# Expert stage of a gated attention and mixture-of-experts block: silu as one function, the row remainder on VectorE, rounding one step earlier, four row buffers, sums formed in the residual's buffer

## The chip, the cores and the metric

The kernel runs on one core of one Trainium2 chip. The metric is device time in microseconds (us) of one execution, the median of several runs. A core has five engines with instruction streams of their own: TensorE (PE, matrix products), VectorE (DVE), ScalarE (ACT), GpSimd (POOL) and SyncE (SP), which here only issues DMAs. They meet through semaphores alone. SBUF holds tiles of 128 partitions; PSUM holds what TensorE writes.

## What is computed

The inputs are 128 sequences of 128 rows of 256 numbers. A gated window attention gives x1. What the change touches is the second half:

```
x = x + tanh(g_xattn[0]) * attention(layernorm(x), ctx)            # x1
x = x + tanh(g_ffn[0]) * ffn(layernorm(x), ...)

def ffn(x, w_router, w_fc, w_gate, w_proj):        # E = 16 experts, K = 2
    gate_probs = softmax(x @ w_router)
    top_k_probs, positions, indices, expert_inputs = dispatch(x, gate_probs)   # 16 rows of a sequence to each expert
    gg = einsum('enc,ech->enh', expert_inputs, w_gate)
    h  = einsum('enc,ech->enh', expert_inputs, w_fc)
    h  = silu(gg) * h
    o  = einsum('enh,ehc->enc', h, w_proj)
    return sum over k of top_k_probs[k] * o[indices[k], positions[k]]
```

All of it is in fp32 accuracy: an operand of a product is split into a rounded head (`_hi`) and a remainder (`_lo`), and three products stand for one.

## The kernel before

Three blocks run one after the other: attention (to about 1310 us of the trace), routing (to about 1340), and the expert block, which the change is in. Attention and routing leave in DRAM the normed rows `xn2_d` and the residual `x1_d`, and in SBUF the tables `place`, `collect_row` and `weight`.

The expert block is a pipeline of steps u = -13 to 141. A step does one unit of each stage, and each stage has a lag: it works at step u on sequence (or expert pair) u minus its lag. The lags are `LOAD -13` (SP fetches the rows of a sequence), `PICK -11` (ACT rounds them to `x_hi`, POOL forms `x_lo`, DVE the selection matrix `pick`), `DISPATCH -9` (PE sorts rows to experts into `DS`, ACT and DVE split that into `s_hi`, `s_lo`), `GATE 0` (PE multiplies by both first weights into `GU`; ACT and DVE form silu(g)*h), `HIDDEN 2` (PE transposes into `HT`, ACT and DVE split it), `OUTPUT 3` (PE multiplies into `EO`, ACT copies it to `eo` and stores it to `eo_d`), `FETCH 12` (POOL gathers the two expert rows of each row of a sequence, `first` and `second`, by an indirect DMA each; SP loads the residual `xr`), and `COLLECT 14` (DVE adds both, weighted, to the residual in `y_sb`; SP stores it). Eight units of GATE to OUTPUT work on one group of eight sequences, two experts each, so a gather of a group waits until all sixteen experts' rows of the group have landed in `eo_d`.

Within a step each engine's instructions stand in the order in which the code is written; nothing is scheduled. All buffers are small rings: three for `x_in_sb` and `xr` (slices of one tile named `scaled`, which the trace shows for both and for `y_sb`), two for `y_sb`, `x_hi`, `x_lo` and the PSUM tiles, three for `eo`, `first` and `second`. So a transfer or an instruction also waits for the last reader of its slot:

- L1129 to L1133, SP: the load for sequence n waits until `x_hi` and `x_lo` of n-3 are done, and stands behind the store of the same step (L1124 to L1126), which waits for `out_done`.
- L1151, POOL: a pair of gathers waits until the sum of n-3 is done; the gathers are followed by `x_lo` (L1162).
- L1188 to L1190, ACT: `x_hi` waits for its load, and the tanh of GATE (L1195) stands behind it.
- L1228 and L1243, DVE: the two sums, with `th` and `hid` (L1235, L1239) between them; the first waits for both gathers, for the residual, and for the store of n-2.

silu(g)*h is computed as (1 + tanh(g/2)) * g * h, with the missing half put into `weight` by the routing block.

## Time and profile before

| what | value |
|---|---|
| median of 3 runs | 1836.87 us (1833.91 to 1838.42) |
| the profiled execution's own time | 1835.99 us |
| its span, first to last instruction | 1834.2 us |
| PE / DVE / ACT / POOL busy over the span | 83% / 77% / 62% / 59% |
| expert block | 1340 to 1834 us |
| its steps without sums (before 1402 us) | PE busy all the time |
| its steps with sums (1402 to 1758 us) | DVE busy 91 to 94%, POOL 80 to 85%, PE 87 to 95% |
| its end (1800 to 1834 us) | gathers on POOL, sums on DVE |

A share of busy time is a mean over unlike stretches. The last third of the run is the expert block, and in it a step is the unit to think in: it has 24 matmuls on PE (12 for GU, 4 for DS, 6 for EO, 2 for HT), so that a count of matmuls in a stretch, divided by 24, is a count of steps.

### The profile page before, as it was taken

Reading aid. Unit: us, or ns where it says so; the run is one execution under the profiler, and the core shown is the slowest. Engines: PE = TensorE matmul, PEld = TensorE weight load, DVE = VectorE, ACT = ScalarE, POOL = GpSimd, SP = SyncE. Lnnn points to the kernel's source line nnn. Section 1 sums busy time; section 2 is a strip of 40 time slices with the busy share of each in tenths; the row PEclk is TensorE's granted clock in tenths of the full one; section 3 lists DMA queues with packets and bytes.
Section 4 is the critical chain, followed back from the end, with each engine's and each line's share of the span. In section 5 each row is a group of like instructions: output and inputs, shape, how many; then the busy total and the mean of one; then the engine's idle time right before and its main releaser. Section 6 shows DMA issues by size and latency. Waiting matters only on the chain. (4 is left out here: it accounts for less than half of the span.)

```text
span 1834.2 us, 50716 instructions
## 1 busy us (share of the span) xinstructions
PE 1520.0 (83%) x16843; PEld 1222.3 (67%) x16844; DVE 1410.9 (77%) x2993; ACT 1133.7 (62%) x2321; POOL 1088.1 (59%) x1490
## 2 busy tenths in 40 slices
PE   4888889988899898898988989986169888898871
PEld 3666666666666666666666666664059888898871
DVE  3777787777877777777777777775968999999964
ACT  3667667677666766766766767674236555565540
POOL 3455465555655555555555555551826888788866
PEclk9999999999999999999999999997569999999995
DMA  2112122121221211212212122242026888898876
GB/s 90 48 58 86 57 71 72 57 86 57 69 74 57 85 58 57 86 57 73 70 57 86 57 70 73 70 145 81 6 72 198 260 263 261 262 286 269 263 228 207
DMA packets 156096, 210.21 MB, mean 115 GB/s; under 512 B 18688, under 2 KB 104832, under 8 KB 156032
## 3 DMA queue, kind: packets, MB, share of 16 engines
q1 hardware_dynamic: 125312, 142.36, 24.5%
q0 software_dynamic: 12288, 33.57, 6.4%
q10 hardware_dynamic: 18432, 33.56, 5.1%
q8 instruction: 24, 0.39, 0.1%
q14 instruction: 40, 0.33, 0.1%
HBM read 125.54 MB, written 83.89 MB: 114 GB/s over the span
## 5 line engine op out<-in xcount | busy, mean ns | idle before, releaser
L505 DVE TRANSPOSE_TENSOR_REDUCE part_max<-ST 128x16 f32<-128x512 f32 x512 | 321.3, 685 | 171.9 <-PE ST L684 168.4
L360 ACT ACTIVATE probs_t<-ST 128x512 f32<-128x512 f32 x512 | 262.5, 596 | 68.2 <-PE ST L699 68.2
L711 PE MATMUL PO<-probs_t,v_aug 128*32 128x128 f32 x4096 | 205.2, 298 | 108.6 <-ACT probs_t L360 95.0
L288 POOL TENSOR_TENSOR ct_lo<-c_in_sb,ct_hi 128x512 fp32r<-128x512 f32 x64 | 82.4, 1288 | 278.0 <-ACT ct_hi L378 278.0
L711 PEld LDWEIGHTS PO<-probs_t,v_aug 128*32 128x32 f32 x4096 | 94.4, 114 | 204.5 <-ACT probs_t L360 192.6
L437 ACT ACTIVATE xn<-x_in_sb,off,rstd 128x256 f32<-128x256 f32 x128 | 70.0, 594 | 224.7 <-POOL off L284 224.7
L1190 ACT ACTIVATE x_hi<-scaled 128x256 fp32r<-128x256 f32 x128 | 53.5, 418 | 210.9 <-DMA scaled<-xn_d 131.9
L1259 PE MATMUL GU<-we_hi,s_hi 128*128 128x256 f32 x512 | 155.8, 304 | 0.0
L1153 POOL DMA_INDIRECT first<-eo_d,collect_row x128 | 126.0, 984 | 44.4 <-issue 24.0
L316 POOL TENSOR_TENSOR q_rest<-q_rot,q_head 128x512 f32<-128x512 f32 x64 | 82.4, 1288 | 112.7 <-ACT q_head L413 112.7
L1153 POOL DMA_INDIRECT second<-eo_d,collect_row x128 | 122.6, 958 | 42.3 <-issue 38.7
L1260 PE MATMUL GU<-we_hi,s_lo 128*128 128x256 f32 x512 | 145.2, 284 | 0.0
L1261 PE MATMUL GU<-we_lo,s_hi 128*128 128x256 f32 x512 | 145.1, 283 | 0.0
L1162 POOL TENSOR_TENSOR x_lo<-scaled,x_hi 128x256 fp32r<-128x256 f32 x128 | 115.2, 900 | 48.8 <-ACT x_hi L1190 46.7
L1259 PE MATMUL EO<-we_hi,h_hi 128*128 128x256 f32 x256 | 82.5, 322 | 53.2 <-issue 39.4
L366 ACT ACTIVATE out_t<-PO 128x512 f32<-128x512 f32 x128 | 78.6, 614 | 71.0 <-PE PO L711 71.0
L729 PE MATMUL F<-ident_sb,xn 128*128 128x128 f32 x512 | 91.8, 306 | 31.6 <-ACT xn L437 19.7
L679 PE MATMUL ST<-q_hi,k_hi 32*128 32x256 f32 x1024 | 94.6, 358 | 5.9 <-issue 5.4
L1260 PEld LDWEIGHTS GU<-we_hi,s_lo 128*128 128x128 f32 x512 | 98.6, 192 | 0.0
L1261 PEld LDWEIGHTS GU<-we_lo,s_hi 128*128 128x128 f32 x512 | 98.1, 192 | 0.0
L1259 PEld LDWEIGHTS GU<-we_hi,s_hi 128*128 128x128 f32 x512 | 97.9, 191 | 0.2 <-issue 0.2
L1259 PEld LDWEIGHTS EO<-we_hi,h_hi 128*128 128x128 f32 x256 | 49.0, 191 | 72.9 <-issue 63.2
(158 smaller groups left out, 5565.7 us busy)
## 6 DMA issues: line engine op xcount, KB each, us to landing
eo_d<-eo ACTq DMA_DIRECT2D x128, 256.0 KB
x_in_sb<-x SPq DMA_DIRECT2D x64, 256.0 KB, 2.8
c_in_sb<-ctx_t SPq DMA_DIRECT2D x64, 256.0 KB, 2.8
xr_sb<-x SPq DMA_DIRECT2D x64, 256.0 KB, 4.0
x_d<-x SPq DMA_DIRECT2D x64, 256.0 KB, 4.1
xn_d<-xn SPq DMA_DIRECT2D x64, 256.0 KB, 4.2
scaled<-xn_d SPq DMA_DIRECT2D x128, 128.0 KB
scaled<-x_d SPq DMA_DIRECT2D x128, 128.0 KB
```

The costliest lines, as they stand in the source:

```text
L288: pool.tensor_tensor(ct_lo[:].rearrange("p k b t -> p (k b t)"), c_in_sb[:, n.par].rearrange("p k b t -> p (k b t)"), ct_hi[:].rearrange(" ...
L316: pool.tensor_tensor(q_rest[:].rearrange("p k t -> p (k t)"), q_rot[:].rearrange("p k t -> p (k t)"), q_head[:].rearrange("p k t -> p (k t ...
L360: act.activation(probs_t[:, b, i].rearrange("p j q -> p (j q)"), ST[i][:], ACT.Exp) \
L505: dve.tensor_reduce(part_max[:, i, 0], ST[i][:].rearrange("p (c l) -> p c l", l=32), AX_X, ALU.max, apply_transpose=True).then_inc(M["part ...
L679: pe.matmul(ST[i][:, m * 2 * SEQ:(m + 1) * 2 * SEQ], k_part[rows, n.par, m, b], q_part[rows, n.par, m, b].rearrange("p e t -> p (e t)"), s ...
L711: last = pe.matmul(PO[32 * j:32 * j + 32, i * SEQ:(i + 1) * SEQ], v_aug[:, n.par, b, head], probs_t[:, b, i, j], start=True, stop=True)
L729: last = pe.transpose(F[:, (2 * k + b) * SEQ:(2 * k + b + 1) * SEQ], src[:, b, k * P:(k + 1) * P], ident[:])
L1153: pool.indirect_dma_start(out=dst[:, n.turn(3)], out_offset=None, in_=D["eo_d"][n.group].rearrange("r e c -> (r e) c"), in_offset=bass.Ind ...
L1162: pool.tensor_tensor(x_lo[:, n.slot(2)], x_in_sb[:, n.turn(3)], x_hi[:, n.slot(2)].bitcast(F32), ALU.subtract).then_inc(M["x_lo_done"], 1)
L1259: pe.matmul(out, lh, rh, start=first, stop=False)
L1260: pe.matmul(out, ll, rh, start=False, stop=False)
L1261: return pe.matmul(out, lh, rl, start=False, stop=last)
```

## The change

- The tanh and the two products become one Silu on ACT and one product on DVE, in place in a tile `gate`. `weight` is no longer halved.
- `x_lo` moves from POOL to DVE, in front of `pick`. POOL has only gathers left in this block.
- `x_hi` moves one step ahead of `x_lo` and `pick` (`HEAD -11`, `PICK -10`), with a ring of four.
- `LOAD` goes from -13 to -14, `FETCH` from 12 to 13, `COLLECT` from 14 to 15. There is one more step at either end.
- `x_in_sb` and `xr` have four slots each. The sums are written over the residual in `xr`, and `y_sb` is gone: the load of a residual now waits until the store of n-4 has landed.
- On SP a step is now load, residual, store, where it was store, load, residual. On ACT `h_hi` stands ahead of the copy of `EO`. On DVE the product of GATE stands ahead of both sums, and `s_lo` between them.

DVE, one step in the middle of the block; `th`, `hid` and `gate` belong to GATE, the two rows that write `scaled` are the sums. Before:

```order
L1249 TENSOR_TENSOR s_lo<-DS,s_hi 128x32x16
L1213 TENSOR_TENSOR h_lo<-HT,h_hi 128x256
L1218 TENSOR_TENSOR pick<-logits,iota_sb 128x256
L1228 SCALAR_TENSOR_TENSOR scaled<-first,weight,scaled 128x256
L1235 SCALAR_TENSOR_TENSOR th<-th,GU 128x256
L1239 TENSOR_TENSOR hid<-th,GU 128x256
L1243 SCALAR_TENSOR_TENSOR scaled<-second,weight,scaled 128x256
```

and in the changed kernel:

```order
L1206 TENSOR_TENSOR h_lo<-HT,h_hi 128x256
L1212 TENSOR_TENSOR x_lo<-scaled,x_hi 128x256
L1214 TENSOR_TENSOR pick<-logits,iota_sb 128x256
L1223 TENSOR_TENSOR gate<-gate,GU 128x256
L1228 SCALAR_TENSOR_TENSOR scaled<-first,weight,scaled 128x256
L1234 TENSOR_TENSOR s_lo<-DS,s_hi 128x32x16
L1239 SCALAR_TENSOR_TENSOR scaled<-second,weight,scaled 128x256
```

`th` is gone, `x_lo` has come, and `s_lo` has moved between the sums.

SP, where the first stores begin. Before:

```order
L1137 DMA scaled<-x_d 128x256
L1132 DMA scaled<-xn_d 128x256
L1137 DMA scaled<-x_d 128x256
L1126 DMA out<-scaled 128x256
L1132 DMA scaled<-xn_d 128x256
```

and in the changed kernel:

```order
L1131 DMA scaled<-x_d 128x256
L1126 DMA scaled<-xn_d 128x256
L1131 DMA scaled<-x_d 128x256
L1136 DMA out<-scaled 128x256
L1126 DMA scaled<-xn_d 128x256
```

The cycle of the three is the same one; what moved is where a step begins in it, and so which sequence each of them serves when it comes up: a load no longer waits behind the store of its own step.

The diff, cut to its core:

```diff
-        then(dve.tensor_scalar(weight[:], prob[:], gates[:, 3:4], 0.5, ALU.mult, ALU.mult))
+        then(dve.tensor_scalar(weight[:], prob[:], gates[:, 3:4], None, ALU.mult))
...
-    LOAD, PICK, DISPATCH, GATE, HIDDEN, OUTPUT, FETCH, COLLECT = -13, -11, -9, 0, 2, 3, 12, 14
+    LOAD, HEAD, PICK, DISPATCH, GATE, HIDDEN, OUTPUT, FETCH, COLLECT = -14, -11, -10, -9, 0, 2, 3, 13, 15
...
-    x_in_sb, xr, y_sb = tiles[:, 0:3], tiles[:, 3:6], tiles[:, 6:8]
-    x_hi = sb("x_hi", [P, 2, DIM], F32R)
+    x_in_sb, xr = tiles[:, 0:4], tiles[:, 4:8]
+    x_hi = sb("x_hi", [P, 4, DIM], F32R)
...
     @block.sync
     def _(sp):
         def step(unit, on):
+            n = unit(LOAD)
+            if on(LOAD):
+                wait_for(sp, M["x_hi_done"], n.n - 3)
+                wait_for(sp, M["x_lo_done"], n.n - 3)
+                sp.dma_start(x_in_sb[:, n.turn(4):n.turn(4) + 1], D["xn2_d"][:, bass.ds(n.n, 1)]) \
+                    .then_inc(x_in[n.turn(4)], 16)
+            n = unit(FETCH)
+            if on(FETCH):
+                wait_for(sp, y_out[n.turn(4)], (n - 4).landed(4))
+                sp.dma_start(xr[:, n.turn(4):n.turn(4) + 1], D["x1_d"][:, bass.ds(n.n, 1)]) \
+                    .then_inc(x1_in[n.turn(4)], 16)
             n = unit(COLLECT)
             if on(COLLECT):
                 sp.wait_ge(M["out_done"], n.n + 1)
                 sp.dma_start(D["out"][bass.ds(n.n, 1)].rearrange("b t c -> t b c"),
-                             y_sb[:, n.slot(2):n.slot(2) + 1]).then_inc(y_out[n.slot(2)], 16)
-            n = unit(LOAD)
-            if on(LOAD):
-                wait_for(sp, M["x_hi_done"], n.n - 2)
-                wait_for(sp, M["x_lo_done"], n.n - 2)
...
-            n = unit(FETCH)
-            if on(FETCH):
-                wait_for(sp, M["y_part_done"], n.n - 2)
...
     def _(pool):
...
-            n = unit(PICK)
-            if on(PICK):
-                pool.wait_ge(M["x_hi_done"], n.n + 1)
-                wait_for(pool, M["ds_done"], n.n - 1)
-                pool.tensor_tensor(x_lo[:, n.slot(2)], x_in_sb[:, n.turn(3)], x_hi[:, n.slot(2)].bitcast(F32),
-                                   ALU.subtract).then_inc(M["x_lo_done"], 1)
...
     def _(act):
...
-            n = unit(PICK)
-            if on(PICK):
-                act.wait_ge(x_in[n.turn(3)], n.landed(3))
-                wait_for(act, M["ds_done"], n.n - 1)
+            n = unit(HEAD)
+            if on(HEAD):
+                act.wait_ge(x_in[n.turn(4)], n.landed(4))
+                wait_for(act, M["ds_done"], n.n - 3)
...
-                wait_for(act, M["hid_done"], n.n - 1)
-                act.activation(th[:, n.slot(2)], GU[n.slot(2)][:].rearrange("p (e f n) -> p e f n", e=2, f=2)[:, :, 0],
-                               ACT.Tanh, scale=0.5).then_inc(M["th_done"], 1)
+                wait_for(act, M["ht_done"], n.n - 1)
+                act.activation(gate[:, n.slot(2)], GU[n.slot(2)][:].rearrange("p (e f n) -> p e f n", e=2, f=2)[:, :, 0],
+                               ACT.Silu).then_inc(M["gate_done"], 1)
...
     def _(dve):
...
             n = unit(PICK)
             if on(PICK):
+                dve.wait_ge(M["x_hi_done"], n.n + 1)
                 wait_for(dve, M["ds_done"], n.n - 1)
+                dve.tensor_tensor(x_lo[:, n.slot(2)], x_in_sb[:, n.turn(4)], x_hi[:, n.turn(4)].bitcast(F32),
+                                  ALU.subtract).then_inc(M["x_lo_done"], 1)
...
+            n = unit(GATE)
+            if on(GATE):
+                gu = GU[n.slot(2)][:].rearrange("p (e f n) -> p e f n", e=2, f=2)
+                dve.wait_ge(M["gate_done"], n.n + 1)
+                dve.tensor_tensor(gate[:, n.slot(2)], gate[:, n.slot(2)], gu[:, :, 1], ALU.mult).then_inc(M["hid_done"], 1)
             n = unit(COLLECT)
             if on(COLLECT):
...
-                wait_for(dve, y_out[n.slot(2)], (n - 2).landed(2))
-                dve.scalar_tensor_tensor(out=y_sb[:, n.slot(2)], in0=first[:, n.turn(3)],
-                                         scalar=weight[:, 0, bass.ds(n.n, 1)], in1=xr[:, n.turn(3)],
+                dve.scalar_tensor_tensor(out=xr[:, n.turn(4)], in0=first[:, n.turn(3)],
+                                         scalar=weight[:, 0, bass.ds(n.n, 1)], in1=xr[:, n.turn(4)],
                                          op0=ALU.mult, op1=ALU.add).then_inc(M["y_part_done"], 1)
```

## Rows read from the trace of the kernel before

**Rows 1.** Busy time by stretch: us, busy (instructions) by engine, PE clock, DMA share, GB/s

```profile
core 0: us, PE busy (x) PEld busy (x) DVE busy (x) ACT busy (x) POOL busy (x), PEclk, DMA share, GB/s
1370.00:1400.00 30.00, 30.00 (x250) 29.80 (x249) 22.95 (x53) 20.37 (x53) 11.68 (x15) 1.00 0.45 150
...
1500.00:1550.00 50.00, 43.54 (x343) 41.08 (x342) 47.01 (x102) 28.73 (x73) 41.49 (x44) 1.00 0.84 261
...
1610.00:1650.00 40.00, 38.29 (x300) 36.06 (x300) 36.86 (x88) 23.84 (x62) 34.02 (x39) 1.00 0.93 288
```

**Rows 2.** All of line 1243, the second sum: duration min/median/max ns, first and last start

```profile
L1243 DVE SCALAR_TENSOR_TENSOR scaled<-second,weight,scaled x104: 477/701/1066, 1402.5 to 1758.6; 128x256 f32<-128x256 f32 x104
```

**Rows 3.** DVE's timeline, one step: start us, us, instruction, [idle before it and releaser]

```profile
1504.25 1.06 DVE L1243 SCALAR_TENSOR_TENSOR scaled<-second,weight,scaled 128x256 f32<-128x256 f32 x1
1505.23 0.68 DVE L1249 TENSOR_TENSOR s_lo<-DS,s_hi 128x512 fp32r<-128x512 f32 x1
1505.84 0.41 DVE L1213 TENSOR_TENSOR h_lo<-HT,h_hi 128x256 fp32r<-128x256 f32 x1
1506.17 0.41 DVE L1218 TENSOR_TENSOR pick<-logits,iota_sb 128x256 fp32r<-128x256 f32 x1
1506.53 0.48 DVE L1228 SCALAR_TENSOR_TENSOR scaled<-first,weight,scaled 128x256 f32<-128x256 f32 x1
1506.93 0.41 DVE L1235 SCALAR_TENSOR_TENSOR th<-th,GU 128x256 f32<-128x256 f32 x1
1507.38 0.42 DVE L1239 TENSOR_TENSOR hid<-th,GU 128x256 f32<-128x256 f32 x1
1507.71 1.01 DVE L1243 SCALAR_TENSOR_TENSOR scaled<-second,weight,scaled 128x256 f32<-128x256 f32 x1
```

**Rows 4.** POOL's timeline of the same step

```profile
1503.94 0.94 POOL L1153 DMA_INDIRECT second<-eo_d,collect_row  x1 [0.30 <-issue]
1504.89 1.02 POOL L1162 TENSOR_TENSOR x_lo<-scaled,x_hi 128x256 fp32r<-128x256 f32 x1
1506.09 0.96 POOL L1153 DMA_INDIRECT first<-eo_d,collect_row  x1 [0.18 <-issue]
```

**Rows 5.** DVE's and POOL's timelines, a step of the faster stretch

```profile
1612.52 0.48 DVE L1243 SCALAR_TENSOR_TENSOR scaled<-second,weight,scaled 128x256 f32<-128x256 f32 x1
1612.91 0.68 DVE L1249 TENSOR_TENSOR s_lo<-DS,s_hi 128x512 fp32r<-128x512 f32 x1
...
1612.52 0.94 POOL L1153 DMA_INDIRECT second<-eo_d,collect_row  x1 [0.30 <-issue]
1613.48 0.74 POOL L1162 TENSOR_TENSOR x_lo<-scaled,x_hi 128x256 fp32r<-128x256 f32 x1
```

**Rows 6.** Who waited for whom, 1450 to 1700 us: total, times, longest

```profile
ACT x_hi L1190 <- DMA scaled<-xn_d: 58.1, 39, 2.7
```

**Rows 7.** A load on SP's queue, and the x_hi on ACT that waits for it

```profile
1505.78 0.45 SPq L1132 DMA_DIRECT2D scaled<-xn_d  x1
...
1509.88 0.42 ACT L1190 ACTIVATE x_hi<-scaled 128x256 fp32r<-128x256 f32 x1 [1.67 <-DMA scaled<-xn_d]
```

**Rows 8.** Store and residual load on SP, and the sum two steps later, with its longest wait

```profile
1748.54 0.34 SPq L1126 DMA_DIRECT2D out<-scaled  x1
...
1749.41 0.62 SPq L1137 DMA_DIRECT2D scaled<-x_d  x1
...
1754.48 0.87 DVE L1228 SCALAR_TENSOR_TENSOR scaled<-first,weight,scaled 128x256 f32<-128x256 f32 x1 [1.29 <-issue]
```

**Rows 9.** ACT by line, 1450 to 1700 us: busy us, mean ns

```profile
L1195 ACT ACTIVATE th<-GU 128x256 f32<-128x256 f32 x73 | 26.8, 367 | 0.0
```

**Rows 10.** The only table load of the run: duration ns, start us

```profile
L351 ACT ACT_TABLE_LOAD  x1: 1283/1283/1283, 0.7 to 0.7; - x1
```

**Rows 11.** DVE's timeline at the end: two first sums, nine apart

```profile
1808.64 0.48 DVE L1228 SCALAR_TENSOR_TENSOR scaled<-first,weight,scaled 128x256 f32<-128x256 f32 x1 [1.32 <-DMA scaled<-x_d]
...
1831.00 0.48 DVE L1228 SCALAR_TENSOR_TENSOR scaled<-first,weight,scaled 128x256 f32<-128x256 f32 x1 [1.81 <-DMA second<-eo_d,collect_row]
```

More of the change, by code:

```diff
@@ L1065, in expert_block @@
     s_lo = sb("s_lo", [P, 2, KC, EXPERTS, GROUP, CAP], F32R)
-    th = sb("th", [P, 2, 2, HID])
-    hid = sb("hid", [P, 2, 2, HID])
+    gate = sb("gate", [P, 2, 2, HID])
     h_hi = sb("h_hi", [P, 2, 2, P], F32R)
@@ L1077, in expert_block @@
     w_down = [T[w][:, KC * half:] for w in ("we_hi", "we_lo")]
-    names = ("x_hi_done x_lo_done pick_done ds_done s_hi_done s_lo_done gu_done th_done "
-             "gated_done hid_done ht_done h_hi_done h_lo_done eo_done eo_copied y_part_done out_done").split()
+    names = ("x_hi_done x_lo_done pick_done ds_done s_hi_done s_lo_done gu_done gate_done "
+             "hid_done ht_done h_hi_done h_lo_done eo_done eo_copied y_part_done out_done").split()
     M = {n: sem(n) for n in names}
-    x_in = [sem(f"xn2_in{r}") for r in range(3)]
+    x_in = [sem(f"xn2_in{r}") for r in range(4)]
     rows_in = [sem(f"rows_in{r}") for r in range(3)]
-    x1_in = [sem(f"x1_in{r}") for r in range(3)]
+    x1_in = [sem(f"x1_in{r}") for r in range(4)]
     eo_out = [sem(f"eo_out{r}") for r in range(3)]
-    y_out = [sem("y_out0"), sem("y_out1")]
+    y_out = [sem(f"y_out{r}") for r in range(4)]
     DS = [pb("DS0"), pb("DS1")]
@@ L1169, in step @@
         def step(unit, on):
-            n = unit(OUTPUT)
-            if on(OUTPUT):
-                act.wait_ge(M["eo_done"], n.n + 1)
-                wait_for(act, eo_out[n.turn(3)], (n - 3).landed(3))
-                act.activation(flat(eo[:, n.turn(3)]), EO[n.slot(2)][:], ACT.Copy).then_inc(M["eo_copied"], 1)
             n = unit(HIDDEN)
@@ L1182, in step @@
             if on(OUTPUT):
+                act.wait_ge(M["eo_done"], n.n + 1)
+                wait_for(act, eo_out[n.turn(3)], (n - 3).landed(3))
+                act.activation(flat(eo[:, n.turn(3)]), EO[n.slot(2)][:], ACT.Copy).then_inc(M["eo_copied"], 1)
+            n = unit(OUTPUT)
+            if on(OUTPUT):
                 act.wait_ge(M["eo_copied"], n.n + 1)
@@ L1250, in step @@
                                   tokens(s_hi, n).bitcast(F32), ALU.subtract).then_inc(M["s_lo_done"], 1)
+            n = unit(COLLECT)
+            if on(COLLECT):
+                dve.wait_ge(M["y_part_done"], n.n + 1)
+                dve.scalar_tensor_tensor(out=xr[:, n.turn(4)], in0=second[:, n.turn(3)],
+                                         scalar=weight[:, 1, bass.ds(n.n, 1)], in1=xr[:, n.turn(4)],
+                                         op0=ALU.mult, op1=ALU.add).then_inc(M["out_done"], 1)
         run_flat(dve, step)
@@ L1279, in step @@
                 for e in range(2):
-                    last = pe.transpose(HT[n.slot(2)][:, e * P:(e + 1) * P], hid[:, n.slot(2), e], ident[:])
+                    last = pe.transpose(HT[n.slot(2)][:, e * P:(e + 1) * P], gate[:, n.slot(2), e], ident[:])
                 last.then_inc(M["ht_done"], 1)
@@ L1300, in step @@
                 wait_for(pe, M["s_lo_done"], n.n - 1)
+                slot = n.slot(4)
                 for k in range(KC):
                     out = DS[n.slot(2)][:, k * SLOTS:(k + 1) * SLOTS]
-                    pe.matmul(out, x_hi[:, n.slot(2), k * P:(k + 1) * P], pick[:, n.slot(2)], start=True, stop=False)
+                    pe.matmul(out, x_hi[:, slot, k * P:(k + 1) * P], pick[:, n.slot(2)], start=True, stop=False)
                     last = pe.matmul(out, x_lo[:, n.slot(2), k * P:(k + 1) * P], pick[:, n.slot(2)],
```

28 lines of the change are left out of this document (5 added, 23 removed).

## The prediction

> **What bounds the kernel now.** I read the busy time by stretch first [rows 1]. A step has 24 matmuls, so the count of matmuls gives the pace. Before any sums are formed, 250 matmuls in 30 us are a step every 24 x 30 / 250 = 2.88 us, with PE busy all of it: PE alone sets that pace. From 1500 to 1550 us, with sums, 343 matmuls in 50 us are 3.50 us a step; from 1610 to 1650 us it is 3.20. Over all of that stage the second sum runs 104 times, from 1402.5 to 1758.6 us [rows 2], so 103 steps take 356.1 us, or 3.457 us each. PE is no longer the bound there. The question is what costs 0.58 us a step.
>
> Three things are late together. **DVE** has no gap at all in a slow step [rows 3]. From start to start its instructions take 0.98 (second sum), 0.61 (`s_lo`), 0.33 (`h_lo`), 0.36 (`pick`), 0.40 (first sum), 0.45 (`th`) and 0.33 (`hid`): 3.46 us. The second sum is the odd one. It takes 1.06 us when it starts 0.31 us into the gather `second` and `x_lo` follows on POOL [rows 3, 4]; it takes 0.48 us when it and the gather start together at 1612.52 [rows 5]. In the slow case it ends 0.43 us after the gather does (1504.88), so it was held until then. The first sum, beside a gather that another gather follows, takes 0.48 us at the same sort of offset (0.44 us) [rows 3, 4]. I read this as DVE and POOL's two-input `x_lo` claiming the same access to SBUF, with `x_lo` already queued behind the gather. `x_lo` pays too: 1.02 us against 0.74 [rows 4, 5].
>
> **POOL** is full as well: gather, gap, gather, `x_lo`, from 1503.94 to the next `second` at about 1507.4, is 3.42 us [rows 4]. In the faster stretch the same cycle is 3.2 us, and that is the pace there.
>
> **The load of x_hi** is the third. The load is issued after the store of its step, at 1505.78, and `x_hi` starts at 1509.88, having waited 1.67 us for it [rows 7]; ACT waited so 39 times, 58.1 us in all [rows 6]. The tanh stands behind `x_hi`, and `th`, `hid` and the second sum behind the tanh. From the end of the second sum (1505.31) to `x_hi` is 4.57 us; with 0.42 for `x_hi`, 0.37 for the tanh [rows 9], 0.78 on DVE and about 1.0 for the sum that closes it, the loop over two steps is 7.1 us, 3.6 a step. Cutting one of the three would leave the others. The change touches all three.
>
> **The change, part by part.**
>
> *DVE.* `th` goes (-0.45). `x_lo` comes; no row has it on DVE. The nearest are `h_lo` and `pick`, two-input instructions of the same size, at 0.33 and 0.36 from start to start; the upper bound is the 0.48 of a first sum. I take 0.36, that of `pick`, because it too reads both inputs from SBUF. The second sum falls to 0.39 (1612.52 to 1612.91 [rows 5]), since no `x_lo` is queued on POOL. A step is then 0.33 + 0.36 + 0.36 + 0.33 + 0.40 + 0.61 + 0.39 = 2.78 us, below PE's 2.88. The two products no longer wait for each other. The reordering of `s_lo` and the sums costs nothing while DVE has that 0.1 us.
>
> *POOL.* Two gathers with their gaps remain, 0.96 + 0.30 + 0.94 + 0.30 = 2.50 us [rows 4]. That is no bound. A gather pair still waits for the sum of n-3: 2.5 us of issue and a landing like the load's 4.1 us [rows 7] are 6.6, and three steps of 3.05 less 1.5 us (first sum to end of second) are 7.6.
>
> *ACT.* Silu takes the place of the tanh. No row has a Silu; the tanh's 367 ns [rows 9] is the nearest. If it were 0.6 it would still be hidden, as ACT is busy 28.73 of 50 us [rows 1]. The built program has one table load more, at the first Silu, and none after it. The one in the trace takes 1283 ns [rows 10]; I count +1.3 us at the entry, where PE waits for the first products; at best it is hidden. The Trainium skill ("ScalarE: Activation LUTs", section "What ACT_TABLE_LOAD costs") adds a drain of about 1.38 us to each switch of table. By it this term would be 2.7 and the total 1.4 us more. The trace's own load stands at the very start with nothing to drain, so no run here shows it.
>
> *SP and the rings.* A load now waits for `x_lo` early in DVE's step, no longer for the sums, and is used three steps later. That gives it over 8 us for a landing that took 4.1 [rows 7], so ACT's wait is gone. The added wait is the residual's: it may be loaded only when the store of n-4 has landed. Queued behind it on SP are the store of the step and the next load, and the first sum waits for the residual itself. Store and load must together fit into four steps, less 1.5 us from first sum to the end of the second and 0.5 us of issue. At 3.05 us a step that leaves 10.2 us. Two landings like that in rows 7 take 8.2. The worst case is 5.94 from the store and 5.07 from the load to the sum that waited [rows 8], 11.0 us together if each were as late as that. So it costs nothing in most steps and may show now and then.
>
> *Lags.* The sums start one step later and so end one step later. At the end nine sums take 1831.00 - 1808.64 = 22.36 us, 2.5 each [rows 11], set by the gathers. One more of them stands behind PE's end: +2.5 us. The additional step at the start only loads: nothing.
>
> **What is late next.** PE, at 2.88, or the DMA engines. A step moves 896 KB (a 256 KB store of `eo`, two gathers, two loads and a store of 128 KB each), 917.5 kB. The stretch at 3.20 us a step moves 288 GB/s at a DMA share of 0.93; that is 310 GB/s at full share, and the slow stretch gives 261 / 0.84 = 311 [rows 1]. So the DMA engines' floor is 917.5 / 310 = 2.96 us, above PE's. Queues are never quite full, so I take 3.05 us: 97% of it. The bounds are 2.88 and the 3.20 already seen.
>
> **The sum.** 103 steps x (3.457 - 3.05) = 41.9 us less; +2.5 at the end; +1.3 for the table. The span goes from 1834.2 to 1796.1 us. The profiled execution took 1835.99 us, 1.8 more than its span, so 1797.9, or 1798; it lies 0.9 us below the median of the runs, which changes nothing here.
>
> **Rivals.**
>
> *PE is the floor.* If DMAs overlap better than the share says, the step is 2.88 to 2.91 us: 1834.2 - 59 + 3.8 + 1.8 = 1780 to 1784. For it: the stretch without sums runs there [rows 1]. Against: no stretch with sums has less than 3.20. The Trainium skill ("HBM Reference", "Specifications (TRN2)") puts a core that streams alone at about 425 GB/s, by which a step's bytes would need 2.2 us as an estimate, and this rival would be the forecast. The share of 0.93 at 288 GB/s, with transfers of 1 KB rows, speaks against it.
>
> *DMA pressure binds earlier.* Transfers take longer as the share nears one, and every loop over a ring stretches. The pace stays at the 3.20 of the stretch at share 0.93: 1834.2 - 26.5 + 3.8 + 1.8 = 1813.
>
> *The residual's ring becomes the bound, and it is slower.* SP stops at the wait for a store and holds back the next load and store. The step is (store + load + 2.0) / 4. It loses once the two landings exceed 4 x 3.457 - 2.0 = 11.8 us together; at 6.6 us each the step is 3.8, and the kernel takes 103 x 0.34 = 35 us more, about 1875. Only the worst row comes near 11.
>
> *No change.* The gathers hold DVE's two-input instructions even without `x_lo`, as they hold the second sum now. Then the second sum stays near 0.98 and `x_lo` on DVE adds what `th` saved: about 3.4 a step, 1836. Against it: `pick` and the first sum run undisturbed beside `first` [rows 3, 4].
>
> **How the numbers follow.** The forecast of 2.96 to 3.12 us a step has 0.56, PE's floor 0.20, early DMA pressure 0.17, no change 0.03, the ring 0.04. The range 1782 to 1814 takes in most of the first three. A measurement of this kernel tells about 0.3% (5.5 us) from no change: faster 0.93, same 0.03, slower 0.04.
>
> **What would show it.** Right: no second sum over 0.5 us between 1402 us and the end of PE's work; POOL with gaps beside its gathers; a DMA share of 0.95 or more at some 300 GB/s; hardly any wait of `x_hi` for its load; DVE waiting a little in each step. Wrong: SP's residual load issued late after a store, first sums waiting over 1 us for it; second sums still at 1 us; PE without idle time, which is the first rival.

## The result and the profile after

| what | before | after |
|---|---|---|
| median of the runs | 1835.4 us (1833.8 to 1838.4) | 1771.9 us (1770.2 to 1774.4) |
| ratio, 95% interval | | 0.965 [0.963, 0.967] |
| profiled execution / its span | 1835.99 / 1834.2 us | 1770.92 / 1769.1 us |
| step with sums, mean of 103 | 3.457 us | 2.880 us |

The changed kernel is 63.5 us faster. The forecast was 1798 us, 38 us faster: the direction was right, and the time lies 10 us below the range. On one other chip the gain was absent (experiment 6); the cause of that is open.

The changed kernel's busy time by stretch (columns as in [rows 1], which has the same stretch of 50 us before):

```profile
core 0: us, PE busy (x) PEld busy (x) DVE busy (x) ACT busy (x) POOL busy (x), PEclk, DMA share, GB/s
1500.00:1550.00 50.00, 50.00 (x423) 49.99 (x422) 49.21 (x123) 36.10 (x88) 35.00 (x36) 1.00 0.98 321
```

PE is busy all of it: 24 x 50 / 423 = 2.84 us a step, where it was 3.50. DVE is busy 98%, and the DMA engines have a share of 0.98. The second sum's line answers to [rows 2] (duration min/median/max ns, first and last start):

```profile
L1239 DVE SCALAR_TENSOR_TENSOR scaled<-second,weight,scaled x128: 474/478/486, 1406.1 to 1766.4; 128x256 f32<-128x256 f32 x128
```

None of 128 is longer than 486 ns. The row in [rows 2] is not all of its line: it counts the 104 second sums up to 1758.6 us, with a median of 701 ns; over all 128 of the kernel before, the last 24 of them mostly without `x_lo` beside them, it is 575. DVE's timeline of one step answers to [rows 3]:

```profile
1506.39 0.68 DVE L1234 TENSOR_TENSOR s_lo<-DS,s_hi 128x512 fp32r<-128x512 f32 x1
1506.99 0.48 DVE L1239 SCALAR_TENSOR_TENSOR scaled<-second,weight,scaled 128x256 f32<-128x256 f32 x1
1507.38 0.41 DVE L1206 TENSOR_TENSOR h_lo<-HT,h_hi 128x256 fp32r<-128x256 f32 x1
1507.72 0.41 DVE L1212 TENSOR_TENSOR x_lo<-scaled,x_hi 128x256 fp32r<-128x256 f32 x1
1508.05 0.41 DVE L1214 TENSOR_TENSOR pick<-logits,iota_sb 128x256 fp32r<-128x256 f32 x1
1508.40 0.42 DVE L1223 TENSOR_TENSOR gate<-gate,GU 128x256 f32<-128x256 f32 x1
1508.74 0.48 DVE L1228 SCALAR_TENSOR_TENSOR scaled<-first,weight,scaled 128x256 f32<-128x256 f32 x1
1509.13 0.69 DVE L1234 TENSOR_TENSOR s_lo<-DS,s_hi 128x512 fp32r<-128x512 f32 x1
```

From `s_lo` to `s_lo` is 2.74 us, with `x_lo` at 0.33 from start to start. POOL in the same step, against [rows 4]:

```profile
1506.64 0.95 POOL L1152 DMA_INDIRECT second<-eo_d,collect_row  x1 [0.30 <-issue]
1508.24 1.04 POOL L1152 DMA_INDIRECT first<-eo_d,collect_row  x1 [0.65 <-issue]
```

The second sum (1506.99) starts 0.35 us into the gather `second`, the offset at which it was held before, and isn't held. Who waited for whom, 1450 to 1700 us (total, times, longest), against [rows 6]:

```profile
ACT x_hi L1183 <- ACT eo L1173: 40.0, 86, 0.7
POOL first L1152 <- DMA eo_d<-eo: 31.0, 55, 1.0
ACT h_hi L1167 <- PE HT L1271: 30.9, 86, 1.1
```

No `x_hi` waits for its load. ACT and POOL wait; PE and DVE hardly do.

Where the 65.1 us of span went, by the same marks in both traces: the first second sum starts 3.6 us later (1402.5, now 1406.1), of which 2.1 are before the expert block, where nothing changed but a constant; the 103 steps from there take 59.5 us less (356.1, now 296.6); from the 104th sum to PE's end it is 12.3 less (43.8, now 31.5); and from PE's end to the last instruction 3.1 more (31.8, now 35.0).

### The profile page after: what moved, and what is told of

The parts are those of the page before. It is cut to its first block and busy times, and to the rows that moved or that the text cites. A ratio compares the mean times of both kernels' runs of the same rounds, so it can differ in the third digit from the quotient of the medians.

```text
span 1769.1 us, 50462 instructions
## 1 busy us (share of the span) xinstructions
PE 1499.5 (85%) x16844; PEld 1218.0 (69%) x16844; DVE 1372.0 (78%) x2993; ACT 1145.5 (65%) x2322; POOL 977.8 (55%) x1362
## 5 line engine op out<-in xcount | busy, mean ns | idle before, releaser
L1152 POOL DMA_INDIRECT first<-eo_d,collect_row x128 | 132.6, 1036 | 135.7 <-DMA eo_d<-eo 99.0
L729 PE MATMUL F<-ident_sb,xn 128*128 128x128 f32 x512 | 92.4, 308 | 31.5 <-ACT xn L437 19.8
L729 PEld LDWEIGHTS F<-ident_sb,xn 128*128 128x128 f32 x512 | 58.6, 150 | 58.0 <-issue 52.9
L516 DVE TENSOR_TENSOR shift<-PO,own_sb 128x512 fp32r<-128x512 f32 x128 | 88.5, 692 | 4.4
L1234 DVE TENSOR_TENSOR s_lo<-DS,s_hi 128x512 fp32r<-128x512 f32 x128 | 87.8, 686 | 5.1 <-ACT s_hi L1194 4.2
```

The costliest lines, as they stand in the source:

```text
L516: dve.tensor_tensor(shift[:], neg.rearrange("p (o l) -> p o l", o=1).broadcast_to([P, 4 * QB, 32]), own[:].rearrange("p (c o) -> p c o", o ...
L729: last = pe.transpose(F[:, (2 * k + b) * SEQ:(2 * k + b + 1) * SEQ], src[:, b, k * P:(k + 1) * P], ident[:])
L1152: pool.indirect_dma_start(out=dst[:, n.turn(3)], out_offset=None, in_=D["eo_d"][n.group].rearrange("r e c -> (r e) c"), in_offset=bass.Ind ...
L1234: dve.tensor_tensor(tokens(s_lo, n), DS[n.slot(2)][:].rearrange("p (k e s) -> p (k e) s", k=KC, s=CAP), tokens(s_hi, n).bitcast(F32), ALU. ...
```

## The experiments

The kernel before ran beside each on the same chip, and the ratio is to that; the median of that kernel stands behind the other's. Five chips, named A to E here, were used for these runs. The ratio of the changed kernel itself is that of the result: it was not timed again on chips A to D, so a difference between its ratio and that of another row holds what the chips differ by as well, and experiment 6 shows that this can be much. The step is 24 matmuls (26, 18 or 12 where the text says so) times 200 us, over the count of matmuls from 1450 to 1650 us, out of the view by stretch.

| kernel | median / kernel before, us | ratio | step, us | DVE / POOL busy of 200 | DMA share, GB/s |
|---|---|---|---|---|---|
| before | | 1 | 3.44 | 184 / 165 | 0.86, 267 |
| after | 1771.9 / 1835.4 | 0.965 [0.963, 0.967] | 2.87 | 196 / 139 | 0.98, 320 |
| after, `x_lo` on POOL | A: 1846.8 / 1843.2 | 1.003 [1.001, 1.005] | 3.55 | 168 / 165 | 0.83, 258 |
| after, tanh | A: 1820.1 / 1843.2 | 0.987 [0.984, 0.991] | 3.23 | 195 / 123 | 0.89, 285 |
| after, both of these | B: 1846.0 / 1832.0 | 1.008 [1.005, 1.011] | 3.65 | 184 / 161 | 0.82, 252 |
| before, `x_lo` on DVE | A: 1872.5 / 1843.2 | 1.017 [1.013, 1.020] | 3.78 | 170 / 104 | 0.79, 243 |
| before, Silu | A: 1824.1 / 1843.2 | 0.991 [0.987, 0.995] | 3.24 | 164 / 169 | 0.92, 283 |
| before, `x_lo` between gathers | B: 1817.6 / 1832.0 | 0.993 [0.991, 0.995] | 3.34 | 185 / 168 | 0.88, 274 |
| after, old order on SP | C: 1803.3 / 1834.7 | 0.983 [0.980, 0.986] | 3.15 | 178 / 128 | 0.91, 290 |
| after, old order on ACT | C: 1784.4 / 1834.7 | 0.973 [0.969, 0.977] | 3.05 | 182 / 131 | 0.95, 301 |
| after, sums one step earlier | C: 1765.9 / 1834.7 | 0.962 [0.959, 0.965] | 2.88 | 195 / 139 | 0.97, 319 |
| after, 2 matmuls more | D: 1795.2 / 1835.8 | 0.978 [0.975, 0.982] | 3.09 | 182 / 129 | 0.93, 298 |
| after, 128 KB more a step | C: 1782.5 / 1834.7 | 0.971 [0.968, 0.974] | 3.00 | 187 / 133 | 1.03, 350 |
| after, 18 matmuls | D: 1777.6 / 1835.8 | 0.970 [0.966, 0.974] | 2.99 | 184 / 133 | 0.95, 307 |
| the same, 4 gather slots | D: 1761.2 / 1835.8 | 0.959 [0.955, 0.963] | 2.85 | 191 / 141 | 0.98, 321 |
| after, 12 matmuls, one run | B: 1743.4 / 1832.0 | | 2.77 | 142 / 142 | 0.99, 330 |
| the same, 4 gather slots | D: 1735.4 / 1835.8 | 0.945 [0.942, 0.949] | 2.74 | 142 / 144 | 1.01, 335 |
| after, on another chip | E: 1860.5 / 1840.4 | 1.011 [1.009, 1.013] | 3.71 | 151 / 107 | 0.80, 248 |
| the same, sums one step earlier | E: 1859.8 / 1840.4 | 1.010 [1.008, 1.012] | 3.66 | 154 / 109 | 0.81, 251 |

### 1. Undoing a part

`x_lo` back on POOL, all else as changed:

```diff
+            n = unit(PICK)
+            if on(PICK):
+                pool.wait_ge(M["x_hi_done"], n.n + 1)
+                wait_for(pool, M["ds_done"], n.n - 1)
+                pool.tensor_tensor(x_lo[:, n.slot(2)], ...
...
-                dve.tensor_tensor(x_lo[:, n.slot(2)], ...
```

> The changed kernel with the row remainder x_lo back on POOL, behind the two gathers, all else as changed. Theory 1 (the two-input x_lo queued behind a gather holds DVE's sum, and POOL itself is full with it): POOL's cycle is 0.96 + 0.30 + 0.94 + x_lo 0.74 to 1.0 + gaps = 3.2 to 3.4 us a step, so 103 steps cost 0.35 to 0.55 us more each: 1808 to 1828 us; one of the two sums beside the gather that x_lo follows shows stretched runs of up to 1.06 us. Rival (the rings and the order on SP bring the gain, x_lo's engine does not matter): a step stays under 2.95 us, 1772 to 1780 us.

The whole gain is gone; neither theory went so far (1846.8 us, where the first expected 1808 to 1828). The second sum is at a mean of 656 ns again and `x_lo` at 957. But DVE has idle time now (168 us busy of 200), and it is PE that waits for `x_lo`:

```profile
PE DS L1298 <- POOL x_lo L1161: 16.9, 29, 2.0
```

The tanh and its second product back, and `weight` halved again:

```diff
-                               ACT.Silu).then_inc(M["gate_done"], 1)
+                               ACT.Tanh, scale=0.5).then_inc(M["gate_done"], 1)
...
+                dve.scalar_tensor_tensor(out=gate[:, n.slot(2)], in0=gate[:, n.slot(2)], scalar=1.0, in1=gu[:, :, 0],
+                                         op0=ALU.add, op1=ALU.mult).then_inc(M["gated_done"], 1)
```

> The changed kernel with the tanh and two products on DVE in place of Silu and one. DVE's step is 2.75 us in the changed kernel; with th (0.45 us) it is 3.2 us, above PE's 2.84. Theory 1 (DVE is the next bound, all but level with PE): 3.15 to 3.25 us a step, 1772 + 103 x 0.35 = 1808 us (1800 to 1815). Rival (only what was on POOL counted): 1772 to 1778 us.

DVE is full (195 of 200 us) with the sums short (476 ns), and the step is 3.23 us: 2.87 + 0.36. A step of DVE alone, from `s_lo` to `s_lo`, is 3.20 us there. So without Silu DVE is the bound, and Silu is worth 0.36 us a step, some 37 us of 103 steps. The time lies 5 us above the expected 1800 to 1815; outside this stretch the trace has 21.6 us of the waits that experiment 6 comes to.

Both undone, so that only rings, lags and order of the change are left:

> The changed kernel with x_lo on POOL and the tanh with two products: what is left of the change is the rings of four, the lags, the order on SP and ACT, and the order of DVE's instructions. Theory 1 (the loop through the load was as tight as POOL and DVE, and without it those two still set the pace): POOL 3.2 to 3.42 us, DVE 3.2 us or more: 3.2 to 3.45 us a step, 1808 to 1838 us, with hardly any wait of x_hi for its load. Rival (the load's loop was the true bound): 3.0 us or less a step, below 1790 us.

These alone gain nothing; the result is 0.8% slower than before, and 8 us above the range of the first theory. Why it is slower, and not even, is open.

### 2. Doing one part alone

```diff
-                pool.tensor_tensor(x_lo[:, n.slot(2)], ...
...
+                dve.wait_ge(M["x_hi_done"], n.n + 1)
+                dve.tensor_tensor(x_lo[:, n.slot(2)], ...
```

> The kernel before with one edit: x_lo on DVE, ahead of pick. DVE's step is then 3.46 - 0.59 (second sum not held) + 0.34 = 3.2 us and POOL's 2.5. Theory 1: no second sum over 0.5 us, and 3.2 to 3.3 us a step if DVE alone sets it: 1835 - 103 x 0.2 = 1814 us (1808 to 1822). Rival (the loop from second sum over store, load, x_hi and tanh is as tight as DVE): the loop loses only 0.6 us in two steps and x_hi is waited for by DVE as well, so 3.35 to 3.45 us a step, 1825 to 1836 us.

The decisive part, alone, makes the old kernel 1.7% slower; neither theory allowed for that. No sum is held any more (second sums have a median of 478 ns), so contention isn't what costs. Its waits, 1450 to 1650 us:

```profile
POOL first L1153 <- DVE scaled L1240: 49.1, 30, 4.8
...
ACT x_hi L1184 <- DMA scaled<-xn_d: 41.5, 27, 2.0
...
ACT x_hi L1184 <- PE DS L1301: 31.4, 22, 4.5
DVE x_lo L1213 <- ACT x_hi L1184: 21.8, 30, 3.7
```

`x_lo` stands in front of DVE's whole step and waits for an `x_hi` that waits for its load. The row with `PE DS` is the other wait of `x_hi`, for a slot of its ring of two: `x_hi` of n can't be written before PE has read that of n-2. What was a loop beside DVE now runs through it. `HEAD`, the ring of four and the order on SP take it out again: in the changed kernel both of these waits are gone. Of the three only the order on SP was undone by itself (experiment 3), so what `HEAD` and the ring of four do singly is not shown.

Silu alone (the edit of experiment 1, turned round):

> The kernel before with one edit: Silu and one product in place of the tanh and two. POOL's cycle with x_lo stays at 3.2 to 3.42 us. Theory 1 (POOL and DVE are tied together, and DVE's saving of 0.45 us a step turns into waiting): 3.2 us at best, where x_lo is not stretched: 1808 to 1836 us, with second sums still over 0.5 us in part of the steps. Rival (DVE alone was the bound): 3.01 us a step, 1835 - 103 x 0.45 = 1789 us.

The step falls from 3.44 to 3.24 in the profiled execution, but POOL is at 169 of 200 us and the whole gain is under 1%. Only 5 of 109 second sums up to 1757 us are over 0.6 us here, so this step is POOL's cycle and the loop of `x_hi` with hardly any contention. What ACT waits for, 1450 to 1650 us, in the kernel before and here:

```profile
ACT x_hi L1190 <- PE DS L1304: 35.8, 27, 2.1
```

```profile
ACT x_hi L1190 <- PE DS L1301: 60.6, 47, 2.1
```

That is the wait for a slot of `x_hi` again. I had left it out of the prediction, which has the load alone; in the changed kernel, with its ring of four, it is gone.

`x_lo` left on POOL, but between the two gathers:

```diff
                 for k, dst in ((0, first), (1, second)):
+                    if k == 1 and on(PICK):
+                        x_lo_of(unit(PICK))
```

> The kernel before with x_lo issued between the two gathers instead of behind the second. It tells what holds a sum. Theory 1 (a sum is held when it starts some 0.3 us or more into a gather that x_lo follows on POOL): it is now the first sum, beside the gather first, that is stretched, to 0.6 to 1.1 us, and the second sum is 0.48 us. Rival (the second sum is long for a reason of its own, its operands or the gather named second): the second sum stays at a median of 0.70 us and the first at 0.48. The time is within 1.5% of the kernel before under both.

Here the gather `first` is the one that `x_lo` follows. ACT's, POOL's and DVE's timelines, in one step and in another:

```profile
1503.36 0.42 ACT L1194 ACTIVATE x_hi<-scaled 128x256 fp32r<-128x256 f32 x1 [1.20 <-PE DS L1308]
1503.62 0.94 POOL L1161 DMA_INDIRECT first<-eo_d,collect_row  x1 [0.30 <-PE DS L1308]
1504.03 0.96 DVE L1232 SCALAR_TENSOR_TENSOR scaled<-first,weight,scaled 128x256 f32<-128x256 f32 x1 [0.29 <-issue]
1504.57 1.02 POOL L1149 TENSOR_TENSOR x_lo<-scaled,x_hi 128x256 fp32r<-128x256 f32 x1
...
1510.41 0.42 ACT L1194 ACTIVATE x_hi<-scaled 128x256 fp32r<-128x256 f32 x1 [1.32 <-PE DS L1308]
1510.41 0.95 POOL L1161 DMA_INDIRECT first<-eo_d,collect_row  x1 [0.30 <-PE DS L1308]
1510.79 0.47 DVE L1232 SCALAR_TENSOR_TENSOR scaled<-first,weight,scaled 128x256 f32<-128x256 f32 x1
1511.37 0.75 POOL L1149 TENSOR_TENSOR x_lo<-scaled,x_hi 128x256 fp32r<-128x256 f32 x1
```

The first sum was rarely held before the change (5 of 104 over 0.6 us). In the first of these steps it starts 0.41 us into its gather, ends 0.42 us after `x_lo` starts, and takes 0.96 us; `x_lo` takes 1.02. In the second it starts 0.38 us into its gather, with `x_lo` next in order just the same, and takes 0.47; `x_lo` takes 0.75. What differs is `x_hi`, which `x_lo` waits for: it had ended 0.25 us before the sum in the first step and ends 0.04 us after the sum's start in the second. It is so in all of the stage. From 1402 to 1760 us, 88 first sums start beside a gather that `x_lo` follows. 12 are held, and each of them starts 0.06 us or more after that `x_hi` has ended. The other 76 take 0.47 to 0.49 us, and none of them that starts 0.15 us or more into its gather does so more than 0.02 us after the end of `x_hi`. In the kernel before, `x_hi` has always ended by then: there, up to 1760 us, all 66 second sums that start 0.31 to 0.86 us into such a gather are held, and none of the 22 that start in its first 0.25 us.

So the expectation came half true. The sum beside the gather `first` can be held as the other was, which bears out the reading of [rows 3, 4] against the rival; but its median stays at 0.48 us, and 37 of 107 second sums still take over 0.52, most of them beside `x_lo` itself. What holds a sum is not the gather, and not a gather with a two-input instruction next in order, but a gather behind which such an instruction stands with nothing left to wait for.

### 3. Order and lag

SP in the old order of store, load, residual:

```diff
+            n = unit(COLLECT)
+            if on(COLLECT):
+                sp.wait_ge(M["out_done"], n.n + 1)
+                sp.dma_start(D["out"][bass.ds(n.n, 1)].rearrange("b t c -> t b c"),
...
             n = unit(LOAD)
...
-            n = unit(COLLECT)
-            if on(COLLECT):
-                sp.wait_ge(M["out_done"], n.n + 1)
```

> The changed kernel with SP's step in the old order: store, then load, then residual. The load then waits for the store of its step, which waits for the second sum, but the load is still used three steps later. Theory 1 (the lag and the ring of four bring the room, the order on SP adds little): 1770 to 1778 us. Rival (the order matters, the load comes late again): x_hi waits for its load, 3.0 us a step or more, 1785 us or above.

The step is 3.15 us, 0.28 more: the rival came true. First sums wait for their residual, and the gathers for the sums (1450 to 1650 us):

```profile
POOL first L1152 <- DVE scaled L1239: 26.4, 26, 1.5
DVE scaled L1228 <- DMA scaled<-x_d: 21.6, 39, 1.3
```

The copy of `EO` ahead of `h_hi` on ACT, as before the change:

```diff
+                act.activation(flat(eo[:, n.turn(3)]), EO[n.slot(2)][:], ACT.Copy).then_inc(M["eo_copied"], 1)
             n = unit(HIDDEN)
...
-                act.activation(flat(eo[:, n.turn(3)]), EO[n.slot(2)][:], ACT.Copy).then_inc(M["eo_copied"], 1)
```

> The changed kernel with ACT's copy of EO ahead of h_hi, as before. h_lo and so EO's products of the next step come 0.6 us later. Theory 1 (DVE and PE have no slack for it, since both are full): 2.9 to 3.0 us a step, 1778 to 1788 us. Rival (a step of slack covers it): 1770 to 1775 us in the middle, and at the end, where only EO, HT and GU are left, up to 5 us more, as PE waits for h_hi.

The step is 3.05, as the first theory had it. By the ratios, undoing the order on SP costs 1.8% and that on ACT 0.8%, of a gain of 3.5%. On one and the same chip, against the next kernel, which differs from the changed one in its lag alone, they cost 2.1% and 1.0%. The order on SP I had priced at nothing, and that on ACT not at all.

Sums one step earlier:

```diff
-    LOAD, HEAD, PICK, DISPATCH, GATE, HIDDEN, OUTPUT, FETCH, COLLECT = -14, -11, -10, -9, 0, 2, 3, 13, 15
+    LOAD, HEAD, PICK, DISPATCH, GATE, HIDDEN, OUTPUT, FETCH, COLLECT = -14, -11, -10, -9, 0, 2, 3, 12, 14
```

> The changed kernel with FETCH 12 and COLLECT 14 as before: the gathers and sums one step earlier. Theory 1 (one more gather pair stands behind PE's end for each step of lag, 2.5 us, and the room is not needed in the middle): 2 to 3 us less, 1769 to 1770 us. Rival (the gathers of a group then wait for its last store of eo, and the pace suffers every eighth step): 1775 to 1790 us.

This gave 0.962 [0.959, 0.965] and 2.88 us a step, some 6 us less than the changed kernel on its own chip, with intervals that overlap; the comparison side by side is experiment 6.

### 4. Is PE the floor?

A fourth product in EO, 26 matmuls a step:

```diff
+                    last = pe.matmul(EO[n.slot(2)][:, e * DIM:(e + 1) * DIM], h_lo[:, n.slot(2), e],
+                                     w_down[1][:, at:at + DIM], start=False, stop=True)
```

> The changed kernel with two matmuls more a step on PE, of the same shape as the others (a fourth product, remainder by remainder, for each of the two experts of EO): 26 instead of 24. Theory: PE is the floor of the changed kernel, at 2.84 to 2.88 us for 24 matmuls. Then a step takes 26/24 of that, 3.08 to 3.12, in all of the expert block (about 155 steps): about 155 x 0.24 = 37 us more than the changed kernel, 1805 to 1812 us. Rival: the DMA engines or the loop over the gather buffers set the pace and PE only looks full (its weights and matmuls queue up behind them); then PE takes the two into its slack and the time stays within some 10 us of 1772.

```profile
1450.00:1650.00 200.00, 200.00 (x1685) 200.00 (x1684) 182.09 (x455) 133.32 (x325) 129.04 (x130) 1.00 0.93 298
```

26 x 200 / 1685 = 3.09 us a step with PE busy all of it, and 23 us more in all. Two matmuls cost 0.22 of the 0.24 us that the work itself takes. The total falls short of the 37 us expected: the product runs 128 times, not 155, which makes 28 us, and the last 5 us are open. So PE sets the pace of the changed kernel. Experiment 5 shows that it does so by very little.

### 5. What holds a lighter kernel?

Each sum stored twice, 128 KB more a step:

```diff
+                sp.dma_start(D["more_d"][bass.ds(n.n, 1)].rearrange("b t c -> t b c"),
+                             xr[:, n.turn(4):n.turn(4) + 1]).then_inc(y_out[n.turn(4)], 16)
```

> The changed kernel with each sum stored twice: 128 KB more a step (1048.6 kB instead of 917.5), nothing else. Theory 1 (at a share of 0.98 the DMA engines have no room: 328 GB/s at full share): 3.2 us a step, 103 x 0.36 = 37 us more, and more at the end: 1809 us or above. Rival (there is room up to 370 GB/s or more): the step stays at 2.84 to 2.9 us, 1772 to 1780 us.

The step is 3.00 us, between the two theories, at 350 GB/s and a share of 1.03. So 310 GB/s was no ceiling, and 128 KB more a step do cost 0.13 us.

The third product of GU and EO left out, 18 matmuls a step, timed once by itself (1775.9 us, 3.05 us a step) and then in four runs:

```diff
-            pe.matmul(out, ll, rh, start=False, stop=False)
-            return pe.matmul(out, lh, rl, start=False, stop=last)
+            return pe.matmul(out, ll, rh, start=False, stop=last)
```

> The changed kernel without the third product (head times remainder of the weight) in GU and EO, 6 of 24 matmuls of a step left out: PE needs 18 x 0.118 = 2.1 us a step. What is late next sets the pace. Theory 1 (DVE, full at 2.75 us a step, is level with PE): 2.75 us a step, 103 x 0.09 = 9 us less than 1772. Theory 2 (the DMA engines at a share of 0.98 are at their limit of 328 GB/s, 2.80 us): 2.80 us, 4 us less. Both also lose PE time where no sums are formed: 14 steps x 0.1 to 0.7 us, 2 to 10 us.

> The same changed kernel without the third product of GU and EO, with three gather slots, timed in rounds, for comparison with the one with four. If the one look was typical, 1773 to 1779 us at 3.0 to 3.1 us a step; if the lighter PE in fact helps, below 1765.

A quarter of PE's work less, and the step is longer, against both theories: 2.99 us. The same with four slots for each gather buffer (they lie in the space of the weights that aren't read):

```diff
-                wait_for(pool, M["out_done"], n.n - 2)
+                wait_for(pool, M["out_done"], n.n - 3)
...
-                        out=dst[:, n.turn(3)], out_offset=None,
+                        out=dst[:, n.turn(4)], out_offset=None,
```

> The changed kernel without the third product of GU and EO (18 matmuls a step; the heads by the second weights' remainder are left out), and with four slots for each gather buffer in place of three (they lie in the weights' remainder, which this kernel doesn't read). One look at the same kernel with three slots gave 3.05 us a step, first sums waiting for the gather's landing. Theory: what is late there is the loop over the three gather slots: sum of n-3 ends, 0.8 us, two gathers 2.3, landing about 4, first to end of second sum 1.5, together 8.6 to 9.1 us in three steps. With four slots it has four steps, and the step falls to 2.75 (DVE full) to 2.85: about 1755 to 1765 us at the end of which DVE is busy all the time. Rival: the DMA engines are the floor at that mix (share 0.94 to 0.98); then four slots change nothing and the step stays at 3.0 or above.

It is 1.1% faster, and the waits of first sums for their gathers (14.8 us in 200) are gone. First with three slots, then with four:

```profile
DVE scaled L1228 <- DMA second<-eo_d,collect_row: 14.8, 23, 1.5
```

```profile
DVE scaled L1228 <- DMA scaled<-x_d: 8.2, 12, 1.4
```

So the three gather slots are the loop that is nearly as long as PE's step. That they hold the lighter kernel is shown. Why it is then slower than the full one, and not equal, isn't. With four slots the lighter kernel's step is 2.85 us, with DVE busy 191 of 200: no better than the full kernel's 2.87. So PE, DVE and this loop are all but level, and taking work from PE alone gains nothing.

Head by head products alone, 12 matmuls, with `h_lo` and `s_lo` left out, with three and with four slots:

```diff
-            pe.matmul(out, lh, rh, start=first, stop=False)
-            pe.matmul(out, ll, rh, start=False, stop=False)
-            return pe.matmul(out, lh, rl, start=False, stop=last)
+            return pe.matmul(out, lh, rh, start=first, stop=last)
```

> The changed kernel with only head times head in GU and EO, and h_lo and s_lo not formed (12 matmuls a step, 1.5 us; DVE 1.85 us; ACT 2.05 us; POOL 2.5 us): the bytes of a step are the same 917.5 kB. It measures the DMA engines' floor. Theory 1 (my forecast's way to read the share, bytes over share): the floor is 2.8 to 2.96 us a step, 310 to 328 GB/s. Rival (the share of busy time near one is no limit, since packets wait inside it): the step falls to POOL's 2.5 us, 365 GB/s.

> The changed kernel with head by head products only (12 matmuls a step, no h_lo, no s_lo), and four slots for each gather buffer in place of three. With three slots it took 1743 us at 2.77 us a step, DMA share 0.99 and 330 GB/s, first sums waiting 46 us in 200 for the second gather. Neither PE (1.4 us a step) nor DVE (1.8) bounds it. Theory A: the loop over the three gather slots (2.77 x 3 = 8.3 us) is the bound; with four the step falls to about 2.5 (POOL's two gathers) and the rate to 365 GB/s, 1715 to 1725 us. Theory B: the DMA engines are, at about 330 GB/s for this mix; then the step stays at 2.7 to 2.8 and the time at 1740 to 1745.

Here four slots give 2.74 in place of 2.77, and the rate is 335 GB/s. Neither PE nor DVE nor POOL is full. The first sums, which waited for the second gather with three slots, now wait for the residual:

```profile
DVE scaled L1222 <- DMA second<-eo_d,collect_row: 46.0, 44, 2.6
```

```profile
DVE scaled L1222 <- DMA scaled<-x_d: 55.6, 52, 3.0
```

So at this mix of transfers the DMA engines' floor is at most 2.74 us a step, 5% below the changed kernel's. Whether 2.74 is that floor or the loop over the four slots of the residual is not shown: no run gave `xr` a fifth slot.

### 6. The same kernel on another chip

> The changed kernel itself, beside the same kernel with FETCH 12 and COLLECT 14 on one chip: 1768 to 1775 us.

> The changed kernel with the sums one step earlier (FETCH 12, COLLECT 14 as before the change), beside the changed kernel itself. Theory: the step of lag costs one sum more behind PE's end, 2.5 us by the gathers' pace, as the prediction priced it, plus or minus nothing in the stage itself, where PE is full either way: 2 to 3 us less than the changed kernel. The first timing, on another chip, gave 5.9 less, with intervals that nearly touch. Rival: gathers that come one step earlier wait more often for the last store of their group and hold the sums; then it is even or slower.

The changed kernel took 1860.5 us there, 85 us above the range expected, 1.011 [1.009, 1.013] of the kernel before, which took 1840.4, and with the old lags 1859.8, 1.010 [1.008, 1.012]. So the lags make no difference that can be told there, and the changed kernel's gain is not there on every chip. Its step is 24 x 200 / 1294 = 3.71 us. ACT's waits in its trace, 1450 to 1650 us:

```profile
ACT gate L1188 <- remote: 15.9, 10, 1.8
...
ACT h_hi L1167 <- remote: 13.1, 13, 2.3
...
ACT s_hi L1194 <- remote: 9.3, 11, 1.6
```

"remote" is a wait that the profile can put down to nothing on the core. The first trace of the changed kernel has none. Others have a few: the kernel before 7.4 us in all of the expert block, and the four kernels on chip A 7.6 to 25.0 us; from 1450 to 1650 us only the one with the tanh has any, 3.4 us. ACT's timeline shows what it looks like:

```profile
1513.71 0.60 ACT L1194 ACTIVATE s_hi<-DS 128x512 fp32r<-128x512 f32 x1 [0.39 <-remote]
...
1515.21 0.38 ACT L1167 ACTIVATE h_hi<-HT 128x256 fp32r<-128x256 f32 x1 [0.91 <-remote]
...
1524.25 0.39 ACT L1188 ACTIVATE gate<-GU 128x256 f32<-128x256 f32 x1 [1.79 <-remote]
```

The transposes for that `h_hi` had ended at 1512.96. Such stops, single or in twos and threes, come some 7 to 19 us apart, 38.3 us in 200. PE has gaps behind them: its 19 longest waits in that stretch, 0.96 to 2.55 us each, all come 0.9 to 3.6 us after the end of a stop of ACT. Its granted clock in the stretch is 0.97 of 2.4 GHz, with matmuls 0.21 us apart in place of 0.12 for some 3 us after a gap of 2.4 us (at 1.2 GHz, the lower of its two levels, they would be about twice as far apart). PE is idle for 34.5 us of the 200, and is busy 165.5 us with 1294 matmuls that take 154.6 at the first trace's pace (200 us for 1674), 10.9 us more. Together that is 45 us, and the 54 steps there are 0.84 x 54 = 45 us longer than at 2.87. So the loss is PE's gaps and the lower clock after them, and the gaps follow ACT's stops in time; no run takes the stops away. What causes them is open: the trace has no record of it. The kernel before has no trace from that chip, so it is open too whether it has the stops there and bears them, or doesn't have them.

## Why the prediction was right in direction and wrong in size

- **What bounds the kernel now**: right that several things were late together. Undoing `x_lo` alone gives 3.55, doing it alone 3.78. What contention costs apart from POOL's cycle no run shows, since `x_lo` on POOL brings both; and the loop through `x_hi` had a second wait, for its ring of two (35.8 us in 200), that I had not counted.
- **DVE, 2.78 us a step**: 2.74 to 2.75 measured. `x_lo` costs 0.33 where I took 0.36, the sums 0.39 each.
- **POOL, 2.50**: from the gather `second` at 1506.64 to the next at 1509.59 it is busy 1.99 us with 0.30 of a fixed gap and the rest waiting. No bound, as said.
- **Silu and the table load**: Silu takes 0.37 us. The load is hidden, not +1.3 us:

```profile
1361.15 0.41 ACT L1183 ACTIVATE x_hi<-scaled 128x256 fp32r<-128x256 f32 x1
1361.57 1.28 ACT L1188 ACT_TABLE_LOAD   x1
1363.11 0.38 ACT L1188 ACTIVATE gate<-GU 128x256 f32<-128x256 f32 x1 [0.25 <-PE GU L1252]
```

It starts as `x_hi` ends, and after it ACT still waits 0.25 us for PE. The drain of some 1.38 us that the Trainium skill ("ScalarE: Activation LUTs", "What ACT_TABLE_LOAD costs") adds to a switch doesn't show in these rows: from the end of `x_hi` to the Silu is 1.55 us, load and wait for PE together.

- **SP and the rings**: right that the residual's ring costs nothing (no wait of a first sum for `x_d` over 0.2 us from 1450 to 1650), and that the load's wait is gone. But "costs nothing" hid that the order on SP is a part of the gain: the old one costs 0.28 us a step, and the old one on ACT, which has no term, 0.18.
- **What is late next, the step that failed**: I took GB/s over share, 310, for a ceiling and got a floor of 2.96 and a step of 3.05. The changed kernel moves 321 GB/s at 0.98, and with more to store 350 at 1.03. The floor for this mix is 2.74 or less, so it doesn't bind, and the first rival came true: PE's floor, 2.88 in the forecast's terms, 2.88 over the 103 steps, 2.84 in the best stretches. That is 103 x (3.05 - 2.88) = 17.6 us of the 27 between the forecast and the profiled execution (1797.9 and 1770.9). The argument "no stretch with sums has less than 3.20" was drawn from stretches that POOL held; it was no evidence on the DMA engines. The figure of about 425 GB/s that the Trainium skill ("HBM Reference", "Specifications (TRN2)") gives for a core that streams alone pointed to this rival; the highest rate seen here is 350, and no run shows 425.
- **Lags, the term that was missing**: the sum behind PE's end cost 3.1 us, priced at 2.5. But I had left out what lies between the 104th sum and PE's end, and so put it at nothing: it is 12.3 us shorter. PE is busy 6.0 us less there (31.5, now 25.5), with one step less to do, and idle 6.3 us less (12.3, now 5.9). Of the 27, these make 11.7 (12.3, less 3.1, plus the 2.5 of the forecast), less 2.3 at the start (3.6, where 1.3 was forecast).
- **Chances**: the first rival had 0.20, and its time of 1780 to 1784 was 8 to 12 us high for the same reason, the end.

## What to carry to other kernels

Read a ceiling only from a stretch that it bounds: a rate divided by a share, taken where another engine sets the pace, gave 310 GB/s where 335 to 350 were to be had. When several loops have about the same length, an edit's worth depends on the others: here `x_lo` on DVE alone was slower, Silu alone gained under 1%, rings and order alone lost, and together they gave 3.5%. Count every wait of such a loop, its ring as well as its load. And time such a gain on more than one chip: this one was absent on one. That a kernel with PE full and DVE at 98% has no slack left for a stop elsewhere would explain it, but is not shown.
